# First attention: the f16 halves of queries and keys reach the heads' strips through DRAM instead of through products

## The chip, the cores and the metric
One Trainium2 chip, one core. The metric is the device time of one execution in microseconds. A core has TensorE (matrix products, in the traces PE, its weight loads PEld), VectorE (DVE), ScalarE (ACT), GpSimd (POOL) and SyncE (SP), which here only issues DMAs. Each engine works its own list of instructions strictly in order and waits on semaphores; 16 DMA engines move the data.

## The reference, cut to what matters
The whole reference is four layers on x of shape (16, 256, 128): a bucketed attention with an MLP, a dense gated feed-forward of 8 experts, a second attention, and a routed feed-forward. The change touches the first attention alone:

```python
h = _ln(x, ln1_g, ln1_b)
qkv = h @ w_qkv + b_qkv
q, k, v = jnp.split(qkv, 3, axis=-1)          # 16 heads of 8 columns, buckets of 64 tokens
kc = jnp.concatenate([kp, kb], axis=2)        # the bucket before and the own one
scores = jnp.einsum('bnihd,bnjhd->bnhij', qb, kc) * scale
scores = jnp.where(mask, scores, -jnp.inf)
attn = jax.nn.softmax(scores, axis=-1)
ob = jnp.einsum('bnhij,bnjhd->bnihd', attn, vc).reshape(B, T, C)
x = x + ob @ w_out + b_out
h2 = _ln(x, ln2_g, ln2_b)
```

## The kernel before
The first attention (`attention_0`) works on 16 blocks of 256 tokens, one block for each sequence, in a software pipeline. `PARTS_0` is an order written out by hand: an iteration s has four parts (quarters below), each a list of steps with a stage; the step `(what, stage, k)` works on block s - stage. `parts_0` walks the list, and every engine walks the same list and emits its own share of each step. There are 21 iterations (s = 0 to 20). What an engine is given in a quarter it does in the order of that list.

For the block of stage 1 (in iteration s it is block s - 1): `lift` transposes the normalised rows on TensorE into the bank WA, and ScalarE copies them with gain and shift to `hT` (L410), and the attention's output of an older block to `aT` (L412). `qk` forms queries and keys in f32 (L591, L592) in WA; ScalarE writes their upper f16 halves, `high` (L417), and VectorE the rests, `low` (L515). `proj` (L605, L606) then takes 16 products of `high` and `low` with a constant 0/1 matrix `spread`: they lay the 8 columns of each head, three times (high, high, low for queries; high, low, high for keys), into a strip of 32 partitions, so that one product over 32 rows gives q times k to f32 precision. ScalarE copies the results to `qs` (L426) and `ks` (L430); rows 24 and 25 of a strip of `ks` hold ones, for the shift by the row's maximum.

Stage 2: `scores` (L626, with the mask L632) into two banks, VectorE takes maxima (L528), `vproj` forms the values (L611), `mpad` splits the maxima (L536, L537). Stage 3: `shift` transposes the maxima (L638) and VectorE subtracts them from the queries (L543); `weights` forms transposed scores (L648), ScalarE takes the exponential (L438), GpSimd zeroes what lies ahead of the query by a select (L390); `values` (L661) multiplies with the values. ScalarE copies the result to `ots` (`copy`, L443), TensorE transposes it back (`back`, L670), VectorE divides (L551, L552). Stage 4 holds the last values, copy and back of a block. Stage 5: `output` (L682, L684, VectorE L561, L563), and the second norm (`norm2`, ScalarE L449). Stage 6: `halves2`, the f16 halves of the normed rows (ScalarE L458, L461, GpSimd L374). Beside it, for the stage that follows, ScalarE and GpSimd split weights (`split` L466, L468, `wlow` L377). Norms: VectorE `stats` (L498, L502), GpSimd `power` (L348, L349) and, for the second norm, the shift (L369, L371), VectorE `norm` (L508, L510).

SP (L319 to L335) loads the inputs, and paces by `hn_done` 72 stores of a constant tile `blank` to the DRAM tensor `rows`, five for each iteration, and fetches of the dense weights (`fetch_set`).

Of the kernel before, what the change touches and what calls it, by code (L numbers as in the profile page):

```python
# [9 lines left out]
P = 128  # L10
NB, TB, C = 16, 256, 128
T = NB * TB
NT = T // P
# [100 lines left out]
class Lease:  # L114
# [23 lines left out]
    "a32": (F32, (("wq", (P,)), ("wk", (P,)), ("wv", (P,)), ("wo", (P,)), ("cols", (6,)))),  # L138
    "a16": (F16, (("spread", (4, 4, P)), ("ident16", (P,)))),
# [17 lines left out]
def unpacked(m, name):  # L157
# [4 lines left out]
    for part, shape in parts:  # L162
# [19 lines left out]
STAGES_0 = 6  # L182
AHEAD = NB - 2
# [3 lines left out]
def parts_0(step):  # L187

    for s in range(NB + STAGES_0 - 1):
        for part in PARTS_0:  # L190
            for what, stage, k in part:
# [3 lines left out]
                elif what in ("stats", "power", "norm"):  # L195
                    if s < AHEAD + 5:
                        step(what, s, k)
                elif what in ("halves2", "norm2"):
                    if 0 <= s - stage < AHEAD:
                        step(what, s - stage, k)  # L200
                elif what == "split":
                    if 0 <= s - 2 < CUTS:
                        step(what, s - 2, k)
                elif what == "wlow":
                    if 0 <= s - 3 < CUTS:
                        step(what, s - 3, k)
                elif 0 <= s - stage < NB:
                    step(what, s - stage, k)


def attention_0(nc, d, keep, rows, stages):
# [3 lines left out]
    with ExitStack() as ctx:  # L215
# [5 lines left out]
        spread = f16["spread"]  # L221
# [14 lines left out]
        hT = m.sb("hT", [P, BK + TB])  # L236
# [3 lines left out]
        qs = [m.sb(f"qs{p}", [P, 4, TB], F16) for p in range(2)]  # L240
        ks = [m.sb(f"ks{p}", [P, 4, BK + TB], F16) for p in range(3)]
# [18 lines left out]
        gate_in, spread_in = m.sem("gate_in"), m.sem("spread_in")  # L260
# [9 lines left out]
        proj_full, proj_free = m.sem("proj_full"), m.sem("proj_free")  # L270
# [34 lines left out]
        LOADS, CLEARS = 6, 5  # L305
# [11 lines left out]
        def _(sp):  # L317
# [4 lines left out]
            sp.dma_start(a16[:], d["a16"]).then_inc(spread_in, 16)  # L322
            sp.wait_ge(loaded, 16 * LOADS)
            sp.dma_start(x[:, 4:12, :], d["x"][:, 4:12, :]).then_inc(x_mid, 16)
            sp.dma_start(x[:, 12:NT, :], d["x"][:, 12:NT, :]).then_inc(x_rest, 16)
            sp.dma_start(keep["gate0"][:], d["gate0"]).then_inc(gate_in, 16)
            keep["fetch_dense"](sp)
            sp.wait_ge(blank_set, 1)
            for i in range(BLANKS * NC_):
                if i % 10 == 0 and i >= 20:  # L330
                    sp.wait_ge(w_low, i // 5 - 2)
                    keep["fetch_set"](sp, i // 10)
                if i % 5 == 0:
                    sp.wait_ge(hn_done, i // 5 + 1)
                sp.dma_start(blanks[:, i], blank[:]).then_inc(blanked, 16)  # L335
# [61 lines left out]
        def _(act):  # L397
            for dst, src in ((ks[0][:, :, 0:BK], d["kpad"]), (abf[:], d["abf"]), (bv[:], d["b_v"]),
                             (bo[:], d["b_out"].to_broadcast([P, C])),
                             (ks[1][:, :, 0:BK], d["kpad"]), (ks[2][:, :, 0:BK], d["kpad"])):  # L400
# [5 lines left out]
            def step(what, n, k):  # L406
                if what == "lift":
                    act.wait_ge(lift_full, n + 1)
                    if n < NB:
                        ins = act.activation(hT[:, BK:BK + TB], WA[:, 0:TB], ACT.Identity, scale=g1, bias=s1)  # L410
# [9 lines left out]
                if what == "proj":  # L420
                    act.wait_ge(proj_full, n * 4 + k + 1)
                    rows2 = (WA, WB)[k % 2][:].rearrange("p (a i) -> p a i", a=2)
                    if k < 2:

                        wait(act, mt_free, n * 2 - 2)
                        ins = act.activation(qs[n % 2][:, 2 * k:2 * k + 2, :], rows2, ACT.Copy)  # L426
                    else:

                        wait(act, st_full, n * 8 - 16)
                        ins = act.activation(ks[n % 3][:, 2 * k - 4:2 * k - 2, BK:BK + TB], rows2,  # L430
                                             ACT.Identity, bias=cols[:, 5:6])
                    ins.then_inc(proj_free, 1)
# [42 lines left out]
        def _(dve):  # L475
            dve.memset(mpad[:], 0.0).then_inc(cleared, 1)
            dve.memset(hT[:, 0:BK], 0.0).then_inc(cleared, 1)
            sums = Tally(dve, ln, 0, 0)

            def step(what, n, k):  # L480
# [9 lines left out]
                if what == "stats":  # L490
                    wait(dve, rstd_done, n)
                    wait(dve, shift2_done, n - 5)
                    lns = range(4)[both_norms(n)]
                    if n < NB:
                        rows_landed(dve, n)
                    for a in lns:
                        v = x[:, 2 * n + a, :] if a < 2 else keep["x1"][:, 2 * (n - 5) + a - 2, :]
                        sums.inc(dve.bn_stats(st[:, a, :], v))  # L498
                    sums.wait()
                    settle(dve, passed_dve)  # L500
                    for a in lns:
                        ins = dve.bn_aggr(mv[:, a, :], st[:, a, :])  # L502
                        ins.then_inc(var_done, 1) if a == lns[-1] else sums.inc(ins)
                if what == "norm" and n < NB:
# [6 lines left out]
                                      ALU.subtract, ALU.mult).then_inc(hn_done, 1)  # L511
                if what == "low":
                    dve.wait_ge(high_done, n + 1)
                    for a in range(2):
                        ins = dve.scalar_tensor_tensor(out=low[:, a, :], in0=WA[:, a * TB:(a + 1) * TB],  # L515
# [14 lines left out]
                if what == "mpad":  # L530
# [5 lines left out]
                    t.link(dve.tensor_copy(mpad[:, k, :, :, 24], mx[:, k]))  # L536
                    dve.tensor_tensor(mpad[:, k, :, :, 25], mx[:, k], mpad[:, k, :, :, 24],  # L537
                                      ALU.subtract).then_inc(mpad_done, 1)
                if what == "shift":
# [3 lines left out]
                    dve.tensor_tensor(q2[:, k], qs[n % 2][:, :, k * P:(k + 1) * P], MT,  # L543
# [24 lines left out]
        def _(pe):  # L568
# [7 lines left out]
            def step(what, n, k):  # L576
                if what == "lift":
                    wait(pe, lift_free, n)
                    wait(pe, proj_free, min(n * 4 - 1, NB * 4))
# [9 lines left out]
                if what == "qk":  # L589
                    pe.wait_ge(lift_free, n + 1)  # L590
                    pe.matmul(WA[:, 0:TB], wq[:], hT[:, BK:BK + TB], start=True, stop=True)  # L591
                    pe.matmul(WA[:, TB:2 * TB], wk[:], hT[:, BK:BK + TB], start=True,  # L592
                              stop=True).then_inc(qk_full, 1)
                if what == "proj":
                    if n == 0 and k == 0:
                        pe.wait_ge(spread_in, 16)
                    pe.wait_ge(low_done, n + 1)
                    if k == 1:
                        wait(pe, va_done, n)
                        wait(pe, x1_own, n - 3)  # L600
                        wait(pe, h2_done, n - 4)
                    wait(pe, proj_free, n * 4 + k - 1 if k > 1 else 0)
                    for a in range(2):
                        dst, g, w = (WA, WB)[k % 2][:, a * TB:(a + 1) * TB], 2 * (k % 2) + a, k // 2
                        pe.matmul(dst, spread[:, 2 * w, g, :], high[:, w, :], start=True, stop=False)  # L605
                        ins = pe.matmul(dst, spread[:, 2 * w + 1, g, :], low[:, w, :], start=False, stop=True)  # L606
                    ins.then_inc(proj_full, 1)
# [1959 lines left out]
```

## Time and profile before

| | us |
|---|---|
| three runs, median | 1021.27 |
| lowest, highest | 1019.35, 1025.33 |
| the profiled execution | 1019.0 |
| its span on the core | 1017.3 |
| busy in the span: TensorE, VectorE, ScalarE, GpSimd | 926.0, 815.7, 783.2, 434.1 |

The span begins with the first instruction that the profiler saw; the execution's own time is 1.7 us longer. A timeline row gives start, duration, engine, line of the kernel, operation, tiles and the number of instructions merged; in square brackets stands how long the engine was idle before, and what ended it.

### The profile page before, as it was taken

The numbers are of one execution on the slowest core, as the hardware profiler recorded it, in microseconds if no ns is written. First come the engines' busy times: TensorE is split into PE (matmuls) and PEld (weight loads), VectorE is DVE, ScalarE is ACT, GpSimd is POOL, SyncE is SP. The second block draws the span as 40 slices with busy tenths as digits, with TensorE's granted clock in tenths as the row PEclk, the third lists the DMA queues.
The fourth block names the chain that finished last, engine by engine and source line by source line (L and its number), as shares of the span: only waits on it lengthen the run. The fifth ranks groups of instructions, "written<-read, shape, count | busy, mean of one in ns | idle before, by whom it ended". The sixth has DMA issues, their size and how long they took to land. (4 is left out here: it accounts for less than half of the span.)

```text
span 1017.3 us, 29043 instructions
## 1 busy us (share of the span) xinstructions
PE 926.0 (91%) x10222; PEld 593.8 (58%) x10222; DVE 815.7 (80%) x2276; ACT 783.2 (77%) x1546; POOL 434.1 (43%) x613
## 2 busy tenths in 40 slices
PE   5999999978999999999999999778888875899995
PEld 3788888854554444444444444455656554788862
DVE  4888888854877999688889899768888867888845
ACT  3889999978998888888888788367767634788844
POOL 3667777772452000000100001124688767666653
PEclk9999999997999999999999999899999956999998
DMA  8433333101000000222222222011111102323228
GB/s 255 170 132 131 129 132 127 45 19 33 1 2 1 1 1 1 76 81 78 63 73 92 74 73 63 1 56 40 37 54 55 44 28 82 85 82 82 81 59 215
DMA packets 61004, 72.60 MB, mean 71 GB/s; under 512 B 8874, under 2 KB 37804, under 8 KB 60864
## 3 DMA queue, kind: packets, MB, share of 16 engines
q1 hardware_dynamic: 50080, 59.36, 18.8%
q0 software_dynamic: 4544, 8.60, 2.6%
q10 hardware_dynamic: 6240, 2.79, 1.1%
q8 instruction: 86, 1.41, 0.6%
q14 instruction: 54, 0.44, 0.1%
HBM read 40.14 MB, written 31.49 MB: 70 GB/s over the span
## 5 line engine op out<-in xcount | busy, mean ns | idle before, releaser
L922 ACT ACTIVATE d__hf<-keep__banks,dense__d 128x512 f32<-128x512 f32 x288 | 185.8, 681 | 48.3 <-PE keep__banks L1160 47.3
L986 DVE TENSOR_TENSOR d__hl<-d__hf,d__hh 128x1024 f16<-128x1024 f32 x144 | 174.1, 1220 | 28.3 <-ACT d__hh L927 26.0
L906 POOL TENSOR_SCALAR d__rstd<-d__mv 128x4 f32<-128x4 f32 x16 | 14.2, 887 | 336.6 <-DVE d__mv L1114 336.6
L927 ACT ACTIVATE d__hh<-d__hf 128x1024 f16<-128x1024 f32 x144 | 152.2, 1057 | 4.6
L1158 PE MATMUL keep__banks<-dense__xh,dense__w1h 128*128 128x512 f16 x288 | 109.9, 382 | 3.0 <-ACT d__hf L922 1.7
L1158 PE MATMUL keep__banks<-d__hh,dense__w2h 128*128 128x512 f16 x288 | 109.2, 379 | 2.4 <-DVE d__tmp L1043 2.4
L1160 PE MATMUL keep__banks<-dense__xh,dense__w1l 128*128 128x512 f16 x288 | 109.9, 381 | 0.0
L1159 PE MATMUL keep__banks<-dense__xl,dense__w1h 128*128 128x512 f16 x288 | 109.9, 381 | 0.0
L1159 PE MATMUL keep__banks<-d__hl,dense__w2h 128*128 128x512 f16 x288 | 109.2, 379 | 0.0
L1160 PE MATMUL keep__banks<-d__hh,dense__w2l 128*128 128x512 f16 x288 | 109.2, 379 | 0.0
L390 POOL TENSOR_SCALAR_AFFINE_SELECT a__pt<-a__pt 128x512 f32<-128x512 f32 x128 | 83.9, 679 | 52.7 <-ACT a__pt L438 52.4
L1449 POOL DMA_INDIRECT parts<-c__ys,c__dest x78 | 81.0, 1038 | 39.1 <-issue 17.1
L528 DVE TENSOR_REDUCE a__mx<-keep__banks 128x4 f32<-128x512 f32 x128 | 81.8, 681 | 17.0 <-PE keep__banks L632 16.7
L438 ACT ACTIVATE a__pt<-keep__banks 128x512 f32<-128x512 f32 x128 | 69.4, 596 | 12.4 <-PE keep__banks L648 12.2
L1888 POOL DMA_INDIRECT rows<-b__xr,b__slot x64 | 63.9, 998 | 21.5 <-issue 17.0
L1467 ACT ACTIVATE c__hf<-keep__banks,c__bias 128x256 f32<-128x256 f32 x156 | 61.2, 475 | 7.5 <-PE keep__banks L1676 6.6
L1688 PE MATMUL keep__banks<-routed__w2h,c__hh 128*128 x312 | 55.7, 219 | 4.9 <-DVE c__hl L1603 4.1
L1603 DVE TENSOR_TENSOR c__hl<-c__hf,c__hh 128x512 f16<-128x512 f32 x78 | 54.3, 696 | 2.7
L1690 PE MATMUL keep__banks<-routed__w2h,c__hl 128*128 x312 | 55.4, 219 | 0.0
L1689 PE MATMUL keep__banks<-routed__w2l,c__hh 128*128 x312 | 55.4, 219 | 0.0
L1158 PEld LDWEIGHTS keep__banks<-dense__xh,dense__w1h 128*128 128x128 f16 x288 | 30.4, 105 | 35.4 <-ACT d__hf L922 3.2
L1158 PEld LDWEIGHTS keep__banks<-d__hh,dense__w2h 128*128 128x128 f16 x288 | 28.2, 98 | 36.0 <-DVE d__tmp L1043 4.5
(356 smaller groups left out, 2433.6 us busy)
## 6 DMA issues: line engine op xcount, KB each, us to landing
rows<-a__blank SPq DMA_DIRECT2D x72, 268.0 KB, 3.2
d__G<-gates SPq DMA_DIRECT2D x64, 256.0 KB, 3.1
c__xin<-rows SPq DMA_DIRECT2D x39, 134.0 KB, 2.2
dense__stage<-e_w SPq DMA_DIRECT2D x16, 256.0 KB, 3.3
b__stage<-e_w SPq DMA_DIRECT2D x32, 128.0 KB, 2.3
c__yb<-parts SPq DMA_DIRECT2D x8, 256.0 KB, 8.2
c__yb<-parts ACTq DMA_DIRECT2D x8, 256.0 KB, 8.9
out<-c__xo SPq DMA_DIRECT2D x8, 256.0 KB, 2.3
```

What stands on the lines that cost most here:

```text
L390: pool.affine_select(out=v, in_=v, compare_op=ALU.is_ge, fill=0.0, base=BK, pattern=[[0, 8], [1, BK]], channel_multiplier=-1).then_inc(cau ...
L438: act.activation(pt[:, u % 4, :], ST[:, u % 2, :], ACT.Exp, scale=scale).then_inc(exp_done, 1)
L528: dve.tensor_reduce(mx[:, u // 4, :, u % 4], S[:, u % 2, :].rearrange("p (a j) -> p a j", a=4), AX.X, ALU.max).then_inc(s_free, 1)
L922: act.activation(hf[:, q, f], HB[:, f], gelu, scale=1.0 / WS, bias=b1[:, at:at + 1]).then_inc(s_["h_free"], 1)
L927: act.activation(hh[:, j % (LEAD + 1), f - 1:f + 1], hf[:, q, f - 1:f + 1], ACT.Copy).then_inc(s_["hi_done"], 1)
L986: dve.tensor_tensor(hl[:, p, f], hf[:, q, f], hh[:, p, f], ALU.subtract).then_inc(s_["lo%d_done" % i], 1)
L1158: pe.matmul(dst, wh, vh, start=begin, stop=False)
L1159: pe.matmul(dst, wh, vl, start=False, stop=False)
L1160: return pe.matmul(dst, wl, vh, start=False, stop=end)
L1449: pool.indirect_dma_start(parts, bass.IndirectOffsetOnAxis(dest[b % RING][:, a:a + 1], 0), ys[b % RING][:, a, :], None, bounds_check=2 * T ...
L1467: ins = act.activation(hf[b % 2][:, f], HB[:, b % 2, f // 2, f % 2], ACT.Gelu, scale=1.0 / WS, bias=bias[:, f, b:b + 1])
L1888: pool.indirect_dma_start(rows, bass.IndirectOffsetOnAxis(slot[n % SENT][:, k, a:a + 1], 0), words[n % SENT][:, a, :], None, bounds_check= ...
```

## The change
`proj`, its matrix and `qs`, `ks` as results of ScalarE go. SP stores `high` and `low` to a DRAM tensor `heads` of six planes (keys low, keys and queries high twice, queries low, in the order in which the strips take them), three DMAs a block, waits for them, and reads pairs of planes back with a partition step of 4 into a joint tile `kq` (keys and queries), three DMAs a block. A strip's rows are now interleaved: row 4e + c is column e of copy c, and rows 3 and 19 of each 32 hold the ones (`ONE_HIGH`, `ONE_LOW`), set once at the start by three small DMAs over zeroed tiles. Scores wait for the landing. In the list, `lift` moves ahead of `vproj`, and `qk` and `low` move from the second quarter to the first, ahead of `weights` and `copy`; the statistics are cut in two, `xstats` (rows of x) in the first quarter and `stats` (rows of x1) in the third. `hT` becomes two tiles. SP's list is now ordered by block: the stores and loads of a block, then that block's blanks and weight fetches; the rest of x, the first dense weights and the first blanks stand behind block 0's.

```diff
-    "a16": (F16, (("spread", (4, 4, P)), ("ident16", (P,)))),
+    "a16": (F16, (("ident16", (P,)),)),
...
 PARTS_0 = [
-    [("scores", 2, 0), ("vproj", 2, 0), ("shift", 3, 1), ("lift", 1, 0), ("weights", 3, 0), ("values", 4, 3),
-     ("copy", 4, 1)],
-    [("scores", 2, 1), ("mpad", 2, 0), ("qk", 1, 0), ("low", 1, 0), ("output", 5, 0), ("back", 4, 1),
+    [("scores", 2, 0), ("lift", 1, 0), ("vproj", 2, 0), ("shift", 3, 1), ("qk", 1, 0), ("xstats", 0, 0), ("low", 1, 0),
+     ("weights", 3, 0), ("values", 4, 3), ("copy", 4, 1)],
+    [("scores", 2, 1), ("mpad", 2, 0), ("output", 5, 0), ("back", 4, 1),
      ("weights", 3, 1), ("values", 3, 0), ("halves2", 6, 0), ("wlow", 0, 0)],
-    [("scores", 2, 2), ("proj", 1, 0), ("proj", 1, 1), ("shift", 2, 0), ("stats", 0, 0),
+    [("scores", 2, 2), ("shift", 2, 0), ("stats", 0, 0),
      ("weights", 3, 2), ("power", 0, 0), ("values", 3, 1), ("copy", 3, 0)],
-    [("scores", 2, 3), ("mpad", 2, 1), ("proj", 1, 2), ("proj", 1, 3), ("back", 3, 0), ("norm", 0, 0),
+    [("scores", 2, 3), ("mpad", 2, 1), ("back", 3, 0), ("norm", 0, 0),
      ("weights", 3, 3), ("values", 3, 2), ("norm2", 5, 0), ("split", 0, 0)]]
...
+            for n in range(NB):
+                planes = heads[n % 2]
+                sp.wait_ge(high_done, n + 1)
+                wait(sp, landed[n % 2], 48 * (n // 2))
+                for i in (1, 3):
+                    sp.dma_start(planes[i:i + 2].rearrange("s p t -> p s t"), high[:]).then_inc(high_out, 16)
+                sp.wait_ge(low_done, n + 1)
+                sp.dma_start(planes[0:6:5].rearrange("s p t -> p s t"), low[:]).then_inc(low_out, 16)
+
+                sp.wait_ge(high_out, 32 * (n + 1))
+                wait(sp, st_full, n * 8 - 16)
+                for c, pair in enumerate((planes[2:4], planes[0:2], planes[4:6])):
+                    if c == 1:
+                        sp.wait_ge(low_out, 16 * (n + 1))
+                    sp.dma_start(kq[n % 3][c:P:4, :, :, BK:BK + TB].rearrange("r s a t -> r (s a) t"),
+                                 pair.rearrange("s (a r) t -> r (s a) t", a=4)).then_inc(landed[n % 2], 16)
+                if n == 0:
+                    sp.dma_start(x[:, 12:NT, :], d["x"][:, 12:NT, :]).then_inc(x_rest, 16)
+                    keep["fetch_dense"](sp)
+                    sp.wait_ge(blank_set, 1)
+                if n % 2 == 0 and n >= 4:
+                    sp.wait_ge(w_low, n - 2)
+                    keep["fetch_set"](sp, n // 2)
+                for i in range(5 * n, min(5 * n + 5, BLANKS * NC_)):
+                    sp.dma_start(blanks[:, i], blank[:]).then_inc(blanked, 16)
...
                 if what == "qk":
                     act.wait_ge(qk_full, n + 1)
+                    wait(act, high_out, 32 * n)
+                    wait(act, low_out, 16 * n)
...
-                if what == "proj":
-                    act.wait_ge(proj_full, n * 4 + k + 1)
...
                 if what == "lift":
                     wait(pe, lift_free, n)
-                    wait(pe, proj_free, min(n * 4 - 1, NB * 4))
+                    wait(pe, low_done, min(n, NB))
...
-                    pe.wait_ge(proj_free, n * 4 + 4)
+                    pe.wait_ge(landed[n % 2], 48 * (n // 2 + 1))
```

## Rows read from the trace of the kernel before
**Rows 1.** ScalarE's timeline over one full iteration: start, duration, what
```profile
117.31 0.55 ACT L410 ACTIVATE a__hT<-keep__banks,a__a 128x256 f32<-128x256 f32 x1
117.76 0.37 ACT L412 ACTIVATE a__aT<-keep__banks 128x256 f32<-128x256 f32 x1
118.02 1.08 ACT L438 ACTIVATE a__pt<-keep__banks 128x512 f32<-128x512 f32 x2
118.97 0.61 ACT L443 ACTIVATE a__ots<-keep__banks 128x512 f32<-128x512 f32 x1
119.50 0.84 ACT L417 ACTIVATE a__high<-keep__banks,a__a 128x256 f16<-128x256 f32 x2
120.93 1.09 ACT L438 ACTIVATE a__pt<-keep__banks 128x512 f32<-128x512 f32 x2 [0.59 <-PE keep__banks L648]
...
125.54 1.27 ACT L430 ACTIVATE a__ks<-keep__banks,a__a 128x512 f16<-128x512 f32 x2
...
128.12 0.88 ACT L449 ACTIVATE a__hn<-keep__lease,a__shift,a__rstd 128x128 f32<-128x128 f32 x2 [0.30 <-POOL a__shift L371]
...
130.09 0.55 ACT L410 ACTIVATE a__hT<-keep__banks,a__a 128x256 f32<-128x256 f32 x1
```
**Rows 2.** Busy time of each engine in that iteration, then granted clock, DMA share, GB/s
```profile
117.30:130.09 12.79, 12.79 (x330) 10.45 (x318) 11.29 (x34) 11.69 (x25) 9.44 (x17) 1.00 0.47 159
```
**Rows 3.** GpSimd's timeline in the same iteration
```profile
121.69 1.47 POOL L390 TENSOR_SCALAR_AFFINE_SELECT a__pt<-a__pt 128x512 f32<-128x512 f32 x2 [1.65 <-ACT a__pt L438]
123.14 0.67 POOL L374 TENSOR_TENSOR dense__xl<-a__h,dense__xh 128x256 f16<-128x256 f32 x1
123.77 1.16 POOL L377 TENSOR_TENSOR dense__w2l<-dense__stage,dense__w2h 128x512 f16<-128x512 f32 x1
124.88 1.27 POOL L390 TENSOR_SCALAR_AFFINE_SELECT a__pt<-a__pt 128x512 f32<-128x512 f32 x2
126.23 0.19 POOL L348 TENSOR_SCALAR a__rstd<-a__mv 128x4 f32<-128x4 f32 x1
126.51 1.02 POOL L349 TENSOR_TENSOR a__rstd<-a__rstd,a__half 128x4 f32<-128x4 f32 x1
...
127.89 0.20 POOL L371 TENSOR_TENSOR a__shift<-a__shift,a__rstd 128x2 f32<-128x2 f32 x1
```
**Rows 4.** ScalarE's timeline in iteration 17
```profile
206.86 0.36 ACT L412 ACTIVATE a__aT<-keep__banks 128x256 f32<-128x256 f32 x1
...
208.08 0.61 ACT L443 ACTIVATE a__ots<-keep__banks 128x512 f32<-128x512 f32 x1
209.76 1.08 ACT L438 ACTIVATE a__pt<-keep__banks 128x512 f32<-128x512 f32 x2 [1.08 <-PE keep__banks L648]
...
218.48 0.36 ACT L412 ACTIVATE a__aT<-keep__banks 128x256 f32<-128x256 f32 x1
```
**Rows 5.** Busy time of each engine from 212 to 222, columns as in rows 2
```profile
212.00:222.00 10.00, 7.20 (x214) 5.07 (x203) 5.91 (x19) 6.93 (x15) 6.64 (x12) 1.00 0.01 2
```
**Rows 6.** TensorE's timeline: the products of qk
```profile
118.43 0.60 PE L591 MATMUL keep__banks<-a__hT,a__a 128*128 128x256 f32 x2
118.87 0.59 PE L592 MATMUL keep__banks<-a__hT,a__a 128*128 128x256 f32 x2
```
**Rows 7.** SP's timeline: the five blanks of one iteration, issue alone
```profile
128.27 2.62 SPq L335 DMA_DIRECT2D rows<-a__blank  x5
```
**Rows 8.** DMA issues of the whole execution: count, KB each, median us to landing
```profile
c__xin<-rows SPq DMA_DIRECT2D x39, 134.0 KB, 2.2
...
gates<-d__gT SPq DMA_DIRECT2D x1, 128.0 KB, 1.8
...
keep__gate<-gate SPq DMA_DIRECT2D x1, 4.0 KB, 7.3
```
**Rows 9.** Timelines of ScalarE and TensorE at the start
```profile
11.58 0.84 ACT L417 ACTIVATE a__high<-keep__banks,a__a 128x256 f16<-128x256 f32 x2 [2.16 <-PE keep__banks L592]
...
17.82 0.45 PE L626 MATMUL keep__banks<-a__ks,a__qs 32*64 32x128 f16 x16 [0.96 <-ACT a__ks L430]
...
27.09 0.45 PE L626 MATMUL keep__banks<-a__ks,a__qs 32*64 32x128 f16 x16 [0.92 <-ACT a__ks L430]
```
**Rows 10.** Stretch of 2 us at the start, columns as in rows 2
```profile
19.00:21.00 2.00, 2.00 (x28) 1.66 (x27) 1.87 (x4) 0.56 (x1) 0.00 (x0) 1.00 1.05 385
```

More of the change, by code:

```diff
@@ L194, in parts_0 @@
                         step(what, s - 1, k)
-                elif what in ("stats", "power", "norm"):
+                elif what in ("xstats", "stats", "power", "norm"):
                     if s < AHEAD + 5:
@@ L208, in parts_0, with attention_0 @@
                     step(what, s - stage, k)
-def attention_0(nc, d, keep, rows, stages):
+def attention_0(nc, d, keep, rows, heads, stages):
     with ExitStack() as ctx:
@@ L235, in attention_0 @@
         hn = m.sb("hn", [P, 2, C])
-        hT = m.sb("hT", [P, BK + TB])
+        hT = [m.sb(f"hT{p}", [P, BK + TB]) for p in range(2)]
         bv = m.sb("bv", [P, 4, P])
@@ L489, in step @@
                     dve.wait_ge(cleared, CLEARS)
-                if what == "stats":
+                if what == "xstats" and n < NB:
+                    wait(dve, rstd_done, n)
+                    rows_landed(dve, n)
+                    for a in range(2):
+                        sums.inc(dve.bn_stats(st[:, a, :], x[:, 2 * n + a, :]))
+                    sums.wait()
+                    settle(dve, passed_dve)
+                    for a in range(2):
+                        ins = dve.bn_aggr(mv[:, a, :], st[:, a, :])
+                        ins.then_inc(var_done, 1) if a and n < 5 else sums.inc(ins)
+                if what == "stats" and n >= 5:
                     wait(dve, rstd_done, n)
                     wait(dve, shift2_done, n - 5)
[L493 to L498, printed above, removed]
+                    for a in range(2):
+                        sums.inc(dve.bn_stats(st[:, 2 + a, :], keep["x1"][:, 2 * (n - 5) + a, :]))
                     sums.wait()
                     settle(dve, passed_dve)
-                    for a in lns:
-                        ins = dve.bn_aggr(mv[:, a, :], st[:, a, :])
-                        ins.then_inc(var_done, 1) if a == lns[-1] else sums.inc(ins)
+                    for a in range(2):
+                        ins = dve.bn_aggr(mv[:, 2 + a, :], st[:, 2 + a, :])
+                        ins.then_inc(var_done, 1) if a else sums.inc(ins)
                 if what == "norm" and n < NB:
@@ L590, in step @@
                     pe.wait_ge(lift_free, n + 1)
-                    pe.matmul(WA[:, 0:TB], wq[:], hT[:, BK:BK + TB], start=True, stop=True)
-                    pe.matmul(WA[:, TB:2 * TB], wk[:], hT[:, BK:BK + TB], start=True,
+                    pe.matmul(WA[:, 0:TB], wq[:], hT[n % 2][:, BK:BK + TB], start=True, stop=True)
+                    pe.matmul(WA[:, TB:2 * TB], wk[:], hT[n % 2][:, BK:BK + TB], start=True,
                               stop=True).then_inc(qk_full, 1)
[L594 to L607, printed above, removed]
                 if what == "vproj":
-                    pe.wait_ge(proj_free, n * 4 + 4)
+                    wait(pe, va_done, n)
+                    wait(pe, x1_own, n - 3)
+                    wait(pe, h2_done, n - 4)
                     for w in range(4):
-                        ins = pe.matmul(WB[:, w * P:(w + 1) * P], hT[:, w * BK:w * BK + P], wv[:],
+                        ins = pe.matmul(WB[:, w * P:(w + 1) * P], hT[n % 2][:, w * BK:w * BK + P], wv[:],
                                         start=True, stop=True)
```

82 lines of the change are left out of this document (35 added, 47 removed).

## The prediction
> **What bounds the kernel now.** I read the table of stretches first, then each engine's timeline over one iteration of the first attention, because the page's own chain that ended last covers only the later stages. Of the 1017.3 us span only the first 237 us belong to this attention; the rest is not edited. One full iteration runs from the copy of hT at 117.31 to the next at 130.09 [rows 1]: 12.79 us. In it TensorE shows 12.79 us busy, ScalarE 11.69, VectorE 11.29 and GpSimd 9.44 [rows 2]. The first impression is therefore that TensorE is the bound and that taking products off it pays.
>
> The timelines say otherwise. From 121.69 to the end of the shift at 128.09 GpSimd works without a gap: the second causal select, xl, the low half of a weight cut, the third select, and the power for the norms [rows 3]. ScalarE's normalisation waits for it (0.30 at 128.12), the split of the weights follows, and only then comes the next hT copy at 130.09 [rows 1]. And the second select itself waits for the second pair of exponentials (120.93), these for the second weights product, that for the transposes of back, these for ScalarE's copy of ots (118.97), that for the first exponentials (118.02), and these directly follow hT and aT [rows 1]. That closes a ring: hT, exponentials 0, ots copy, back, weights 1, exponentials 1, GpSimd's run, normalisation, split, hT.
>
> The proof that this ring is a limit of its own is iteration 17, which has no scores, lift, qk, low or projection any more. There aT starts at 206.86 and again at 218.48 [rows 4]: still 11.62 us, although TensorE, where it can be seen in 212 to 222, is busy only 7.20 of 10 us [rows 5]. Full iterations add the hT copy (0.45 until aT starts), a power over four columns instead of two (about 0.3, an estimate) and a back that comes 0.28 later (below): 12.65 of the 12.79 seen.
>
> **What the change removes, and what that is worth.** Sixteen half products per block leave TensorE and four ScalarE copies leave as well (the ks pair alone is 1.27 us at 125.54 [rows 1]). They stand in quarters 3 and 4, where the ring runs on GpSimd: it is busy there without a gap, and no GpSimd instruction goes. So this gives nothing while the ring stands; TensorE and ScalarE only wait longer. VectorE's work stays (xstats and stats are one step cut in two, with one more drain, about 0.15 us, off the ring), and the low half keeps its two instructions. The tiles kq cost three memsets and three small DMAs at the start.
>
> **What it moves.** In quarter 1 ScalarE's list becomes lift, qk, weights 0, copy; before, qk stood in quarter 2, behind weights 0 and copy. ScalarE works its list in order, so exponentials 0 now stand behind the high copies, and these behind two f32 products that themselves wait for hT and aT. From the start of hT: hT and aT end 0.82 later (117.31 to 118.13 [rows 1]); hand-over to TensorE 0.1, an estimate (the next hand-over is 0.04); the products 1.03 (118.43 to 119.46 [rows 6]); hand-over 0.04; high copies 0.80 until the next can start [rows 1]. Exponentials 0 start at 2.79 instead of 0.71 (118.02): **+2.08 us**, of which some 1.2 is ScalarE standing idle. Something comes back: from the end of the ots copy to exponentials 1 it is 119.58 to 120.93 = 1.35 today, since back stands in line behind scores, qk and output; with those done early it is what iteration 17 shows, 208.69 to 209.76 = 1.07 [rows 4]: **-0.28**. Queued behind the waiting qk on TensorE are weights 0 and values; behind ScalarE's, the exponentials for which GpSimd waits. The period becomes 12.79 + 2.08 - 0.28 = **14.6 us**, +1.8. Bounds: if back gained nothing +2.1; if half of the qk wait were hidden +1.4.
>
> VectorE has room: 11.29 us of work [rows 2] and some 0.5 of drains in a period of 14.6, and its norm waits for GpSimd's power, not the other way. Its low waits for high, done at hT + 2.83.
>
> **The way through DRAM.** From high done: the second write starts about half a microsecond later (five issues take 2.62 us [rows 7]), the low write starts 0.9 after high and lands 1.8 later (128 KB to DRAM takes 1.8), two more issues 0.5, and a load of 134 KB takes 2.2 [rows 8]: 0.9 + 1.8 + 0.5 + 0.5 + 2.2 = 5.9 us. The next iteration's scores (0.6) and lift (0.8, both estimated from the merged rows of such products) must run before its hT, so the landing is due 1.4 us ahead of it: 14.6 - 2.83 - 1.4 = 10.4 us are free. Hidden, with 4.5 us to spare.
>
> **The start.** High of block 0 is copied at 11.58 (to 12.42) and the first scores start at 17.82 [rows 9]. With 512 KB of spread and the padding not fetched, high may come up to 1.3 us earlier, then 5.9 us: scores 0 at 17 to 18.3, no change. Block 1 is worse: behind the loads of block 0 SP issues the rest of x, the dense weights and five blanks, 3.7 MB; at 385 GB/s [rows 10] and somewhat less for x this drains until about 26 us, while high of block 1 is ready at about 21. The 4 KB gate load, issued behind the same rest of x, took 7.3 us to land [rows 8]. High would land at 27 and the loads at 30, against scores at 27.09 today [rows 9]: +2.9, of which I estimate 2.0 left by iteration 5, as quarters 3 and 4 are shorter there. Bounds -1 to +6.
>
> The Trainium skill has this in "DMA: Bandwidth & Descriptors", section "Queues, rings and completion order": on each DMA engine the descriptors of a queue are consumed in ring order. By that rule the 2.0 for the start stands; without it the start would cost nothing and the sum would be 2 us less. The gate's 7.3 us agree with it.
>
> **Sum.** Iterations 6 to 16 carry the whole ring (11 of them; halves2 begins in 6, the last lift is in 16): 11 x 1.8 = 19.8. Iteration 5 has no xl (0.8 shorter): 13.8 against 12.8, +1.0. Iterations up to 4 have a ring under their other work: 0. Start +2.0. Together +22.8. The profiled execution took 1019.0, so 1041.8; the median of the runs lies 2.3 above it (1019.35 to 1025.33), of which I take half: **1043**. Bounds of the terms: 11 x 1.4 + 0.5 - 1 = +15 to 11 x 2.1 + 1.5 + 6 = +31, that is 1034 to 1053.
>
> **Rivals.**
> *Faster: the ring doesn't bind.* If exponentials 0 did not have to stand behind high, the shorter TensorE and ScalarE lists would count, until VectorE's 11.29 of work [rows 2] with about 0.5 of drains is the limit: 11.8, that is 11 x -1.0 + 2.0 for the start: 1010. It decides from the point where the ring is under 12.8, that is, where the wait for qk is under 0.3. Against it: the order of the list and iteration 17. Chance 0.07.
> *Partly:* ring lengthened by only 0.3 to 1.2, if the ring has slack I don't see: 11 x 0.3 + 3 to 11 x 1.2 + 3, 1025 to 1035. Chance 0.09.
> *The DRAM round binds.* From 10.4 us on, each further one is added to every period; at 12 us it is 1.6 x 14 iterations = 22 more, 1064. Against it: 5.9 from rows. For it: 1536 packets of 512 B a block, of a size that hardly runs in this stretch now. Chance 0.06.
> *TensorE's clock falls* to its lower level, 1.2 GHz, because it now waits. Its work, about 10.8 us, would be over 20: more than 1100. Against it: in 212 to 222 it was busy 72% and granted 1.00 [rows 5]; new, 10.8 of 14.6 is 74%. Chance 0.03. The Trainium skill's "TensorE: Matmul & The Clock Gate", Part 1, says that the clock follows how busy the array has lately been, default low; by it alone these waits would speak for this rival, while the row speaks against.
>
> **Chances.** Forecast 0.74 (1034 to 1053), partly 0.09, DRAM 0.06, clock 0.03, faster 0.07, no change 0.01. Half a per cent, 5 us, is about what a measurement of this kernel can tell from no change. Slower 0.90, same 0.03, faster 0.07. The range 1030 to 1056 holds the forecast, half of partly and little of DRAM: about 0.8.
>
> **What would show it.** In the profile after: hT to hT 14.6 us; ScalarE idle 1.2 before the high copy, released by TensorE's second qk product; the first exponentials 2.8 after hT; GpSimd waits for exponentials about 1.8 longer in all; TensorE busy share in 117 to 200 under 90%; scores never released by a DMA from iteration 4 on, but in iterations 2 and 3 yes. If the period is 11.8 to 12.8, the reading of the ring is wrong; if scores wait for landings in the middle of the stage, the price of the DRAM way is.

## The result and the profile after

The changed kernel takes 1052.87 us in the median (four runs, 1051.13 to 1056.10), the kernel before 1021.18 beside it: a ratio of 1.031 (95% interval 1.027 to 1.035). It is 31.7 us slower. The forecast was 1043, with 1030 to 1056 around it. The profiled execution of the changed kernel is the longest of its four (1056.10), and that of the kernel before (1019.0) is shorter than each of its four; so the spans, 1054.3 and 1017.3, lie 37.0 apart, more than the medians.

All of it lies in the first attention. The first ScalarE instruction of the dense stage starts at 239.01 before and at 275.32 after: 36.3 us later; from there to the end it is 778.3 and 779.0. So the start of hT in each iteration, read from ScalarE's timeline, tells where the time went (the period is the time since the iteration before):

| iteration | before, start (period) | after, start (period) | later by |
|---|---|---|---|
| 2 | 19.74 | 19.89 | 0.15 |
| 3 | 29.25 (9.51) | 38.25 (18.36) | 9.00 |
| 4 | 40.74 (11.49) | 53.89 (15.64) | 13.15 |
| 5 | 53.19 (12.45) | 68.82 (14.93) | 15.63 |
| 6 | 65.98 (12.79) | 82.59 (13.77) | 16.61 |
| 8 | 91.69 (12.79) | 113.28 (16.06) | 21.59 |
| 10 | 117.31 (12.82) | 142.19 (14.46) | 24.88 |
| 16 | 194.38 (12.79) | 229.05 (14.45) | 34.67 |

Two parts stand out: 15.6 us before iteration 5, and then some 1.65 in each iteration, 14.45 for 12.79. The page of the profile after, in its first part (busy us, share, instructions) and in its row of the granted clock in 40 slices, shows TensorE and ScalarE with less work (926.0 and 783.2 before) in more time, VectorE with a little more (815.7 before), and a clock that is not full at the start:

```profile
PE 917.5 (87%) x9966; PEld 576.0 (55%) x9966; DVE 822.5 (78%) x2280; ACT 748.9 (71%) x1482; POOL 431.6 (41%) x613
...
PEclk9598999999799999999999999979999985999999
```

The steady iteration, ScalarE's timeline after, answers rows 1 (start, duration, engine, line, operation, tiles; in brackets the idle time before, and what ended it):

```profile
142.19 0.55 ACT L429 ACTIVATE a__hT<-keep__banks,a__a 128x256 f32<-128x256 f32 x1
142.64 0.37 ACT L431 ACTIVATE a__aT<-keep__banks 128x256 f32<-128x256 f32 x1
144.23 0.84 ACT L438 ACTIVATE a__high<-keep__banks,a__a 128x256 f16<-128x256 f32 x2 [1.22 <-PE keep__banks L611]
144.96 1.08 ACT L446 ACTIVATE a__pt<-keep__banks 128x512 f32<-128x512 f32 x2
145.91 0.62 ACT L451 ACTIVATE a__ots<-keep__banks 128x512 f32<-128x512 f32 x1
147.61 1.09 ACT L446 ACTIVATE a__pt<-keep__banks 128x512 f32<-128x512 f32 x2 [1.08 <-PE keep__banks L657]
...
149.82 1.08 ACT L446 ACTIVATE a__pt<-keep__banks 128x512 f32<-128x512 f32 x2 [0.22 <-PE keep__banks L657]
...
154.66 0.88 ACT L457 ACTIVATE a__hn<-keep__lease,a__shift,a__rstd 128x128 f32<-128x128 f32 x2 [1.10 <-POOL a__shift L392]
...
156.63 0.55 ACT L429 ACTIVATE a__hT<-keep__banks,a__a 128x256 f32<-128x256 f32 x1
```

ScalarE sits idle for 1.22 us behind aT until the second qk product is there, copies high, and only then takes the first exponentials: 144.96 - 142.19 = 2.77 after hT, where rows 1 have 0.71. From the end of the ots copy (146.53) to exponentials 1 it is 1.08. GpSimd's timeline answers rows 3: it waits 3.43 for those exponentials (1.37 before) and 1.39 for the next pair (1.65 before), and from 148.37 it runs as before without a gap to the shift:

```profile
145.72 1.27 POOL L411 TENSOR_SCALAR_AFFINE_SELECT a__pt<-a__pt 128x512 f32<-128x512 f32 x2 [3.43 <-ACT a__pt L446]
148.37 1.27 POOL L411 TENSOR_SCALAR_AFFINE_SELECT a__pt<-a__pt 128x512 f32<-128x512 f32 x2 [1.39 <-ACT a__pt L446]
149.68 0.67 POOL L395 TENSOR_TENSOR dense__xl<-a__h,dense__xh 128x256 f16<-128x256 f32 x1
150.31 1.15 POOL L398 TENSOR_TENSOR dense__w2l<-dense__stage,dense__w2h 128x512 f16<-128x512 f32 x1
151.42 1.27 POOL L411 TENSOR_SCALAR_AFFINE_SELECT a__pt<-a__pt 128x512 f32<-128x512 f32 x2
...
154.43 0.20 POOL L392 TENSOR_TENSOR a__shift<-a__shift,a__rstd 128x2 f32<-128x2 f32 x1
```

The stretches after, columns as in rows 2, show the steady iteration and the start:

```profile
142.20:156.60 14.40, 11.91 (x303) 8.89 (x302) 11.42 (x34) 9.63 (x21) 9.20 (x17) 1.00 0.51 168
24.00:28.00 4.00, 2.57 (x30) 1.83 (x30) 3.37 (x9) 1.26 (x2) 1.09 (x3) 0.67 1.06 388
28.00:32.00 4.00, 1.23 (x14) 0.53 (x10) 2.51 (x7) 0.00 (x0) 0.00 (x0) 0.50 0.76 251
32.00:36.00 4.00, 0.00 (x0) 0.00 (x0) 0.00 (x0) 0.00 (x0) 0.00 (x0) 0.50 0.39 119
```

In the steady iteration no engine is full. From 32 to 36 every engine is idle; and the granted clock stands at 0.50, the lower level of 1.2 GHz, from 26 to 42. SP's and TensorE's timelines give the halves of block 1 and of a late block:

```profile
25.79 1.55 SPq L337 DMA_DIRECT2D heads<-a__high  x2
27.39 0.50 SPq L339 DMA_DIRECT2D heads<-a__low  x1
31.38 3.02 SPq L346 DMA_DIRECT2D a__kq<-heads  x3
36.57 0.67 PE L635 MATMUL keep__banks<-a__kq 32*64 32x128 f16 x16 [7.34 <-DMA a__kq<-heads]
...
203.05 0.89 SPq L337 DMA_DIRECT2D heads<-a__high  x2
203.99 1.86 SPq L339 DMA_DIRECT2D heads<-a__low  x1
207.02 1.92 SPq L346 DMA_DIRECT2D a__kq<-heads  x3
212.11 0.45 PE L635 MATMUL keep__banks<-a__kq 32*64 32x128 f16 x16 [0.97 <-DMA a__kq<-heads]
```

Block 1's high was copied by 23.54, stored from 25.79, on its way back from 31.38, and used at 36.57; TensorE had waited 7.34 us. The first 2.25 of these 13.0 us are SP's own: it was still issuing blanks (3.39 us for five, from 22.36). In the late block the way takes from 203.03, the end of the high copies, to 212.11: 9.1 us.

### The profile page after: what moved, and what is told of

Same layout as the page of the kernel before. It is cut to its first block and busy times, and to the rows that moved or that the text cites. A ratio compares the mean times of both kernels' runs of the same rounds, so it can differ in the third digit from the quotient of the medians.

```text
span 1054.3 us, 28529 instructions
## 1 busy us (share of the span) xinstructions
PE 917.5 (87%) x9966; PEld 576.0 (55%) x9966; DVE 822.5 (78%) x2280; ACT 748.9 (71%) x1482; POOL 431.6 (41%) x613
## 5 line engine op out<-in xcount | busy, mean ns | idle before, releaser
L411 POOL TENSOR_SCALAR_AFFINE_SELECT a__pt<-a__pt 128x512 f32<-128x512 f32 x128 | 81.5, 660 | 93.6 <-ACT a__pt L446 93.6
L635 PE MATMUL keep__banks<-a__kq 32*64 32x128 f16 x1024 | 31.8, 229 | 20.7 <-DMA a__kq<-heads 18.3
```

What stands on the lines that cost most here:

```text
L411: pool.affine_select(out=v, in_=v, compare_op=ALU.is_ge, fill=0.0, base=BK, pattern=[[0, 8], [1, BK]], channel_multiplier=-1).then_inc(cau ...
```

## The experiments

The theory: a ring through ScalarE's first exponentials and GpSimd's run sets the period, and qk ahead of the exponentials lengthens it. The rivals: the way through DRAM sets it; TensorE's or VectorE's work does.

**The order alone.** The kernel before, with the new first quarter and nothing of the DRAM way.

```diff
-    [("scores", 2, 0), ("vproj", 2, 0), ("shift", 3, 1), ("lift", 1, 0), ("weights", 3, 0), ("values", 4, 3),
-     ("copy", 4, 1)],
-    [("scores", 2, 1), ("mpad", 2, 0), ("qk", 1, 0), ("low", 1, 0), ("output", 5, 0), ("back", 4, 1),
+    [("scores", 2, 0), ("lift", 1, 0), ("vproj", 2, 0), ("shift", 3, 1), ("qk", 1, 0), ("low", 1, 0),
+     ("weights", 3, 0), ("values", 4, 3), ("copy", 4, 1)],
+    [("scores", 2, 1), ("mpad", 2, 0), ("output", 5, 0), ("back", 4, 1),
```

> The kernel before with the new order of the first quarter alone (lift ahead of vproj, qk and low ahead of weights and copy, two hT tiles); the projection by products, qs and ks stay. Theory (ring): the first exponentials stand behind high, so hT to hT goes from 12.8 to 14.4 us in iterations 6 to 16, 11 x 1.65 = 18 us, and the start is as before: about 1039 us. Rival (the DRAM way and its waits are what slows the iterations, the order costs nothing): hT to hT stays 12.8, 1021 us.

Measured: 1047.50 us, ratio 1.024 (1.021 to 1.027). The period from iteration 7 on is 14.45 or 14.46 in every iteration, which is also the changed kernel's in most, with all products, qs and ks still there. ScalarE's timeline (qk, exponentials 0 and the next hT):

```profile
146.01 0.55 ACT L410 ACTIVATE a__hT<-keep__banks,a__a 128x256 f32<-128x256 f32 x1
148.06 0.84 ACT L417 ACTIVATE a__high<-keep__banks,a__a 128x256 f16<-128x256 f32 x2 [1.22 <-PE keep__banks L593]
148.79 1.09 ACT L438 ACTIVATE a__pt<-keep__banks 128x512 f32<-128x512 f32 x2
...
160.47 0.55 ACT L410 ACTIVATE a__hT<-keep__banks,a__a 128x256 f32<-128x256 f32 x1
```

The rival falls. What was not expected: another 6.4 us are lost before iteration 5 (hT at 59.61 for 53.19), though no halves go through DRAM here. The granted clock is 1.00 from 16 to 60 us before, and here 0.51 from 24 to 28, 0.63, 1.00, 0.72 and 0.85 in the next stretches of four. So in the short early iterations too the order costs, and the clock falls with it; how much of the 6.4 is the clock's, no run tells apart.

**Half of the order.** The kernel before with lift ahead of vproj (and two hT tiles) alone; qk and low stay in the second quarter.

> The kernel before with lift ahead of vproj and two hT tiles, but qk and low left in the second quarter: the rest of the order of e1_order_alone. Theory (it is qk ahead of the exponentials that lengthens the ring): hT to hT 12.8 in iterations 6 to 16, and the 7.8 us that e1_order_alone lost before iteration 6 are not lost either, 1021 to 1023. Rival (lift waiting for hn ahead of vproj, and with it VectorE's va, is part of it): 13.2 or more a period, 1027 and up.

Measured: 1026.45 us, ratio 1.007 (1.005 to 1.009), next to the rival's figures. The period is 13.17 from iteration 8 on, 0.37 above the 12.80 before; hT of iteration 5 comes at 51.92, earlier than before, and the clock is 1.00 up to 60 us. So the whole loss before iteration 5 comes with qk's move. Moved by itself, lift costs 0.37 a period, and ScalarE's timeline shows at which step:

```profile
119.20 0.55 ACT L410 ACTIVATE a__hT<-keep__banks,a__a 128x256 f32<-128x256 f32 x1
119.91 1.08 ACT L438 ACTIVATE a__pt<-keep__banks 128x512 f32<-128x512 f32 x2
123.20 1.08 ACT L438 ACTIVATE a__pt<-keep__banks 128x512 f32<-128x512 f32 x2 [0.60 <-PE keep__banks L649]
```

Exponentials 0 come 0.71 after hT, as in rows 1. Exponentials 1 come 3.29 after them, not 2.91: back stands behind scores, qk and output on TensorE, and these start later after hT (scores 0.89 behind it at 120.09, before 0.51 at 117.82). In the order alone that queue is gone: there exponentials 1 come 2.65 after exponentials 0. So these 0.37 are not a part of its 1.65; both moves together cost 1.65, and lift by itself costs 0.37 at a step that the second move makes shorter.

**qk put back.** The changed kernel, qk and low again behind mpad.

> The changed kernel with qk and low put back into the second quarter, behind mpad; halves still go through DRAM. Theory (ring): the order's 1.65 us a period goes. The landing is then next in line: high is done 3.0 after hT, the trip took 8.7 to 9.1 in the trace of the changed kernel, scores and lift need 1.4, so 13.1 to 13.5 us a period instead of 14.45: 11 x 1.1 = 12 us less than 1052.9, about 1041, with TensorE released by DMAs at the scores of every iteration. If the trip shrinks with the order, 12.8 a period and 1035. Rival (the order is not the cause): 14.4 a period, 1053.

Measured: 1065.49 us, ratio 1.046 (1.041 to 1.051): slower than the changed kernel. Three periods (into iterations 13 to 15) are 13.2 to 13.6, next to the 13.1 to 13.5 expected, but by other terms: in the one of 13.33, high is done 3.58 after hT, not 3.0, the way through DRAM takes 7.54, not 8.7 to 9.1, and the next hT comes 2.21 after the scores, not 1.4. The other periods from iteration 4 on are 14.7 to 17.0. Before iteration 5 nothing is won either: its hT comes at 71.14, later than the 68.82 of the changed kernel. TensorE's timeline at scores, and the stretches around two of them:

```profile
99.28 0.67 PE L635 MATMUL keep__banks<-a__kq 32*64 32x128 f16 x16 [3.23 <-DMA a__kq<-heads]
...
177.91 0.45 PE L635 MATMUL keep__banks<-a__kq 32*64 32x128 f16 x16 [1.55 <-DMA a__kq<-heads]
```

```profile
96.00:102.00 6.00, 2.77 (x31) 2.49 (x28) 2.25 (x6) 3.23 (x8) 3.43 (x7) 0.65 0.84 281
176.00:182.00 6.00, 4.45 (x130) 3.80 (x119) 4.34 (x14) 5.03 (x11) 4.29 (x10) 1.00 0.91 308
```

With the ring out of the way each iteration waits for its landing. From the end of the high copies to the scores it takes 7.0 to 10.2 us from block 2 on, 8.5 in the mean (block 1, behind the backlog, 11.9). Where TensorE waits 3.2 us, the clock granted around it is 0.65 and the scores that follow take 0.67 instead of 0.45. The longer period of the changed kernel had hidden this.

**What sets the length of the trip.** High stored once instead of twice (four planes; one store fewer, one load more), qk as above.

```diff
-                for i in (1, 3):
-                    sp.dma_start(planes[i:i + 2].rearrange("s p t -> p s t"), high[:]).then_inc(high_out, 16)
+                sp.dma_start(planes[1:3].rearrange("s p t -> p s t"), high[:]).then_inc(high_out, 16)
```

> qk back in the second quarter as in e2_qk_back, and high stored once instead of twice: four planes, two stores and four loads a block, the loads for the first copy being two of one plane. Theory (the trip binds there, and its length follows the number and volume of stores in front): the pair of high stores took 3.4 to 4.0 us to its last landing, one takes about 0.5 to 0.9 less, so the quiet iterations go from 13.3 to 12.6, and the waits of 3 us that let the clock fall become rarer: about 1050 against 1065.5. Rival (the trip is latency alone, whatever is stored): 13.3 and 1065.

Measured: 1057.62 us, ratio 1.035 (1.029 to 1.040). The trip (the way from the end of the high copies to the scores) is 6.8 to 9.6 us from block 2 on, 8.0 in the mean, so 0.5 shorter, at the lower end of what was expected; the spread is nearly as wide. Its trace is that of the longest of four executions (1053.0 to 1066.1 us).

And all blank stores behind the last block:

> e2_qk_back (qk and low in the second quarter, where the landing binds each iteration) with all 72 blank stores issued after the last block's halves; the total says nothing, since 19 MB of stores then stand at the end of the stage. Looked at: hT to hT in iterations 5 to 16 and the time from the end of the high copies to the scores that the landing releases. In e2_qk_back that was 7.0 to 10.0 us. Theory (the trip varies with what is queued beside it, and the blanks are the most of that): 7 us or less in every iteration, 12.8 a period, clock 1.00. Rival (its length and its spread are the small packets' and the waits' own): 7 to 10 as before, periods of 13.2 to 17.

Measured, in one execution: the trip is 7.2 to 9.8 us from block 1 on, the periods from iteration 5 on 13.7 to 17.5, though the DMA engines are busy only 0.15 to 0.30 of the time between 80 and 200 us. The rival stands: the blanks are not what makes its length or its spread, and one store fewer is worth 0.5. SP's timeline says only where a trip is long: in this run the loads are issued 2.4 to 4.4 us after the high copies are done, once the high stores have landed, issuing the three takes 1.9 to 2.8, and the scores start 1.9 to 3.9 behind the last issue. Block 0 takes 6.4 in the changed kernel, near the shortest of each part. What makes one trip 7.2 and the next 9.5 is open.

**The start.** The rest of x behind block 1 and the blanks from block 2 on:

```diff
                 if n == 0:
-                    sp.dma_start(x[:, 12:NT, :], d["x"][:, 12:NT, :]).then_inc(x_rest, 16)
                     keep["fetch_dense"](sp)
                     sp.wait_ge(blank_set, 1)
+                if n == 1:
+                    sp.dma_start(x[:, 12:NT, :], d["x"][:, 12:NT, :]).then_inc(x_rest, 16)
...
-                for i in range(5 * n, min(5 * n + 5, BLANKS * NC_)):
+                for i in range(max(6 * n - 12, 0), min(6 * n - 6, BLANKS * NC_)):
```

> The changed kernel with SP's queue emptied at the start: the rest of x is loaded behind block 1's halves instead of block 0's, and the blanks begin with block 2, six a block. Theory (of the 16.6 us that hT of iteration 6 comes later, the backlog is the most): high of block 1 finds a queue with the dense weights alone, lands 3 us after it is issued instead of 5.6, its loads at about 30 instead of 36.5: 6 to 8 us less, about 1046. Rival (the trip itself and a lower granted clock are the start's cost, whatever is queued): less than 2 us gained, 1051 or more.

Measured: 1051.72 us, ratio 1.029 (1.026 to 1.031). The scores of block 1 start at 32.54 instead of 36.57 and hT of iteration 5 at 63.13 instead of 68.82: 5.7 us less. In the profiled executions the dense stage starts 5.6 us earlier, 269.76. The whole time shows little of it: the median is 1.2 us lower, which is what the rival expected, and the intervals of the ratios overlap (1.031 for the changed kernel). So the gain is shown for this pair of traces and not for the medians. Of the 13.0 us of block 1's way 8.1 are left: the wait for SP goes from 2.25 to 0.09, the stores take 2.4 instead of 5.6 until the loads are issued, and the loads up to the scores 5.6 instead of 5.2.

TensorE kept at work in the waits for the first two landings:

```diff
+                    if k == 0 and n < 2:
+                        wait(pe, s_free, n * 8 - 1)
+                        for _ in range(WARM[n]):
+                            pe.matmul(S[:, 0, :], identb[:], causal[:].rearrange("p a j -> p (a j)"),
+                                      start=True, stop=True, skip_group_check=True)
```

> The changed kernel with 24 and 30 idle products of 512 columns on TensorE in the two waits for the first landings; they are extra work and change no result. It prices the clock alone: in the changed kernel the granted clock was 0.50 from 26 to 42 us and from 46 to 56. Theory (part of the start is TensorE at the lower of its two levels): the clock stays 1.0 after 18 us and 3 to 5 us are gained, about 1049. Rival (TensorE had slack there, the landing alone sets the time): same, 1052 to 1053.

Measured: 1050.74 us, ratio 1.029 (1.027 to 1.031); hT of iteration 5 at 63.86, 5.0 less. The clock did not stay up as expected (0.73 and 0.50 from 24 to 32), but it was 0.92, 1.00, 0.86 and 0.71 in the stretches of four up to 48 and 1.00 after it, where the changed kernel has 0.50 up to 42 and again from 46 to 56. Here too the intervals of the ratios overlap. The idle products of block 1 run up to its scores (36.81 us, without a wait), so they may have held them up, and the run then prices the clock too low.

Both together:

> The changed kernel with both edits of the start: the quiet queue of e3_start_quiet and the idle products of e4_warm (24 and 16). In those runs hT of iteration 6 came at 76.90 and 77.64 instead of 82.59. If backlog and clock are separate costs the two add: 82.6 - 5.7 - 5.0 = 72 us, and the later iterations stay at 14.45: about 10.6 less than the changed kernel, 1042. If the clock fell only because the wait for block 1's landing was long (one cause, two faces), hT of iteration 6 is at 76 and the time 1046.

Measured: 1049.01 us, ratio 1.027 (1.025 to 1.030); hT of iteration 5 at 60.21, 8.6 less, and of iteration 6 at 75.63, not 72. That is the second reading's 76, though the median is above its 1046 too. It does not show that the two costs overlap: the idle products end only as the scores of block 1 start, at 33.89. The loads were issued by 26.8, and in the two runs with qk put back above the scores start 1.9 to 4.3 us behind the last issue; so by this estimate the halves were there by 31.1, and the products held the scores up themselves. What is left, 60.21, is next to the 59.61 of the order alone, which suggests 6.4 of order and 8.6 of backlog and clock. No run shows that split: with qk put back (above) the start was not shorter, and with qk back and a quiet queue (below) hT of iteration 5 comes at 65.97.

**Another place in the ring.** If the ring is real, a step of GpSimd taken from it shortens both kernels. `wlow` goes from the end of the second quarter to the front of the first.

```diff
-    [("scores", 2, 0), ...
+    [("wlow", 0, 0), ("scores", 2, 0), ...
...
-     ("weights", 3, 1), ("values", 3, 0), ("halves2", 6, 0), ("wlow", 0, 0)],
+     ("weights", 3, 1), ("values", 3, 0), ("halves2", 6, 0)],
```

> The changed kernel with wlow moved in the same way. Theory (ring): in the changed kernel more of it can go, as TensorE has the second weights product earlier: the third select could start 0.76 after 149.82, 150.58 instead of 151.42, so hT to hT is 13.6 instead of 14.45, 12 x 0.84 = 10 us, about 1043. The landing then has 13.6 - 2.9 - 1.4 = 9.3 us and needs 8.7 to 9.1, so it comes close to binding. Rival (the period is set by landings or by VectorE): 14.45 and 1053.

Measured on the changed kernel: 1043.80 us, ratio 1.023 (1.019 to 1.026). The period is 13.60 to 13.62 in seven of the eleven into iterations 6 to 16, 13.94 to 14.45 in the other four. The number expected was 1043; it is met partly by luck, as four periods are longer than expected and hT of iteration 5 comes 2.9 us earlier (65.88), for which nothing was expected.

> The kernel before with one step moved: wlow, GpSimd's low half of a weight cut, from the second quarter, where it stands in the ring between xl and the third select, to the front of the first, where GpSimd is idle for 1.37 us. Theory (the ring through GpSimd sets the period of the kernel before): the third select then starts when its exponential is there, 0.76 after 123.81, so 124.57 instead of 124.88: hT to hT 12.5 instead of 12.8, 11 x 0.3 = 3 us, about 1018.5. Rival (TensorE's 12.79 of 12.79 busy sets it): 12.8 and 1022.

Measured on the kernel before: 1018.14 us against 1020.66, ratio 0.997 (0.995 to 0.999), 0.3% and just clear of no change: the one version here that is faster than both. GpSimd's timeline shows wlow in its idle time and a gap of 0.77 where it stood; below it stand ScalarE's timeline and the stretch from hT to hT:

```profile
118.47 1.16 POOL L377 TENSOR_TENSOR dense__w2l<-dense__stage,dense__w2h 128x512 f16<-128x512 f32 x1
...
124.21 0.67 POOL L374 TENSOR_TENSOR dense__xl<-a__h,dense__xh 128x256 f16<-128x256 f32 x1
125.65 1.27 POOL L390 TENSOR_SCALAR_AFFINE_SELECT a__pt<-a__pt 128x512 f32<-128x512 f32 x2 [0.77 <-ACT a__pt L438]
...
122.01 1.09 ACT L438 ACTIVATE a__pt<-keep__banks 128x512 f32<-128x512 f32 x2 [0.59 <-PE keep__banks L648]
...
123.91 1.07 ACT L426 ACTIVATE a__qs<-keep__banks 128x512 f16<-128x512 f32 x2
124.89 1.09 ACT L438 ACTIVATE a__pt<-keep__banks 128x512 f32<-128x512 f32 x2
...
118.29:130.87 12.58, 12.58 (x326) 10.41 (x318) 11.17 (x35) 11.78 (x25) 9.59 (x17) 1.00 0.49 159
```

Its best periods are 12.58, most 12.7, some 13.1 and 13.3. The median gains 2.5 of the 3 us expected, but where, the trace does not show: it is of the longest of ten executions, and its ten periods into iterations 7 to 16 add up to 128.2, against 128.4 before. What the two periods of 12.58 show is what comes next. The gap says that the third exponentials are then the later of the two, and they stand directly behind the qs copies: from 122.01 to the next hT at 130.87 ScalarE has no wait at all. So from there on ScalarE's own list is the next limit, only 0.3 behind the ring (its wait of 0.30 at 128.12 in rows 1), and there the removed copies would count, though no run tried that. And TensorE shows 12.58 busy of 12.58, as it showed 12.79 of 12.79: its busy time shrank with the period, so it was not what set it.

**All of it together, through DRAM.** qk back, one store, quiet start, wlow moved:

> qk back, high stored once, quiet start, wlow in the first quarter: all that the runs so far suggest for the way through DRAM. If the trip stays at 7.5 us and the clock at its upper level, the period is 12.5 and the start 8 us late: 1028. If the trip varies as in e2_qk_back, 1040. It would have to beat 1022 for the way through DRAM to pay; theory (ring and trip): it does not.

Measured: 1049.35 us, ratio 1.030 (1.024 to 1.035). From iteration 7 on, periods of 12.5 to 13.4 stand beside others of 14.4 to 15.5; the landing releases the scores of every iteration. Expected was 1028 or 1040; it missed both. The start is not 8 us late but 12.8 at hT of iteration 5 (65.97) and 15.3 at that of iteration 6 (81.29), and the ten periods after it are 13.97 in the mean. The trips take 7.0 to 9.1, 7.7 in the mean, so this version exchanges the ring for them.

## Why the prediction was right, and where it was off

**The ring** was right, step by step. First exponentials after hT: 2.79 forecast, 2.77 measured; ots copy to exponentials 1: 1.07 and 1.08; idle before high 1.2 and 1.22; period 14.6 and 14.45. So every sign named for the ring came, with GpSimd's longer waits too (2.06 - 0.26 = 1.80, forecast 1.8). The missing 0.15 lies in GpSimd: in rows 3 the second select pair took 1.47, now 1.27, and xl starts 2.07 behind exponentials 1 (147.61 to 149.68) instead of 2.21. Eleven periods at 1.65 more cost 18.1 instead of 19.8, iteration 5 cost 0.98 against 1.0. That the removed products and copies gave nothing is what the order alone shows: 14.45 with them and without. Moving lift was costed at nothing; by itself it costs 0.37 (half of the order), but at a step that the whole order takes out, and the steps above add up to the 1.65 without it. The removed copies would count only in a kernel whose ring is some 0.3 shorter (wlow moved), where ScalarE's own list is the limit.

**The start** was mis-sized: +2.0 forecast, with bounds of -1 and +6; +15.6 measured. Three steps failed. High of block 1 was expected at 21 and was ready at 23.5. Its way through the backlog and back was put at 9 us and took 13.0 (23.54 to 36.57). The quiet queue brings the scores of block 1 from 36.57 to 32.54, 4.0 earlier. The rule of the Trainium skill that the prediction cites ("DMA: Bandwidth & Descriptors", "Queues, rings and completion order"), that descriptors of a queue are consumed in ring order, agrees with that: stores issued behind the backlog took 5.6 us until the loads could follow, without it 2.4. And "iterations up to 4 have a ring under their other work: 0" was wrong: in the kernel before, the order alone costs 6.4 there. How the 15.6 divide between order, backlog and clock stays open.

**The clock** was a rival with a chance of 0.03, for the whole stage. It came in part: 0.50 to 0.67 between 24 and 42, again 0.50 from 46 to 56, and once in the middle, where iteration 7 to 8 took 16.06 instead of 14.45 (0.50 from 94 to 100). The steady iterations kept 1.00 (142 to 157), but with TensorE busy 11.91 of 14.40, 83% and not the 74% forecast; the comparison with the 72% of rows 5 said nothing of the uneven ones. The Trainium skill says that the clock follows how busy the array has lately been ("TensorE: Matmul & The Clock Gate", Part 1), and the traces agree: from 92 to 94 TensorE was busy 0.97 of 2.00 us and the clock stood at 0.50 after it.

**The way through DRAM** was put at 5.9 us and takes 7 to 10 where it can be seen; only block 0 comes near, with 6.4. In the late block above it is 4.0 until the high stores have landed (203.05 to 207.02), where the terms of the forecast give 0.5 + 1.8 = 2.3, and 5.1 from there to the scores, where they leave 3.6. Median times to landing are 2.2 and 2.9 us for 128 KB, not 1.8 and 2.2 as rows 8 had. It was hidden all the same, since 10.4 was put as free. But the sign named for it, that no scores are released by a DMA from iteration 4 on, failed: five scores after iteration 5 were, by 0.50 to 0.97 us. After the longest of these waits, ahead of 212.11, the period was still 14.45, so it cost nothing there. The rival "the DRAM round binds" was right about the versions with qk put back.

The sum: 18.1 + 1.0 + 15.6 + 1.6 for the one slow iteration = 36.3, in the profiled execution; the forecast was 22.8, with +31 as the upper end of its terms. In the medians the difference is 31.7: the profiled execution of the changed kernel is 3.2 above its median and that of the kernel before 2.2 below its own. Which part of the kernel differs between executions no trace shows, and it stays open. So 1052.87 inside 1034 to 1053 is in part luck: the ring came as forecast, and the start, far outside its bounds, was made up for by the room in the ring's (2.1 a period, 1.65 measured) and by the medians, which lie closer together than the profiled executions.

## What to carry to other kernels

When every engine looks nearly full, look for an iteration that lacks most of the work: if its period is hardly shorter, suspect a ring of hand-overs, follow it step by step, and move one step out of it as a test; while it binds, removing work from the fullest engine gives nothing. In an in-order list a step that waits is paid by everything behind it, so put it behind the steps that others wait for. Two dependent DMAs in a loop are free only while the loop is longer than their slowest passage.

## What the runs showed of the hardware

- Three stores of 128 KB in rows of 512 B to DRAM, waited for, and their reload by three loads take 7.0 to 10.2 us from one block to the next (qk put back), and as much (7.2 to 9.8) with the blanks gone and the DMA engines busy 0.15 to 0.30 of the time.
- TensorE's granted clock fell to 0.50 behind short waits: with the order alone it waited 1.83 us ahead of 24.05 and worked at the lower level from there. In the changed kernel it fell near 94 us, after a wait of 1.03.
- At the very start the granted clock in the rows reads 1.00 while the products say otherwise: before, the f32 products of qk take 1.22 and 1.06 us at 9.47 and 10.48, and 0.60 and 0.59 at 118.43 and 118.87. With the order alone the eight products of vproj still take 1.92 at 18.59, where the kernel before takes 1.06 at 18.43.
- At the lower level the same products take 1.5 to 2 times as long (scores 0.67 for 0.45, vproj 1.91 for 1.06, the first qk product pair 1.17 for 0.70 in the changed kernel). The one iteration in the middle in which it fell took 16.06 instead of 14.45, and from 100 to 102 the clock was back at 0.90. Whether a fallen clock makes the waits that keep it down was not tested.
